# Attention units in a mixed attention and expert kernel: the product with V a pair later, three probability buffers, even units normalised by ScalarE and VectorE, and a shorter check of the low halves

## The reference, cut to what matters

```python
q, k, v = (layernorm(x) @ (codes * scales) + b)          # [16, 256, 16 heads, 128]
scores = einsum('bqhd,bkhd->bhqk', q, k) / sqrt(128)
attn = softmax(scores, axis=-1)
out = einsum('bhqk,bkhd->bqhd', attn, v) @ (wo_codes * wo_scales) + bo
x = x + layernorm(out)
logits = layernorm(x) @ gate.T                           # softmax, best 3 of 8 groups, best 6 experts
y = sum_k topk_w[k] * expert_k(layernorm(x)) + shared(layernorm(x))
x = x + layernorm(y)
```

## Time and profile before

| | value |
|---|---|
| three timed runs | 1329.47, 1331.55, 1333.42 us (median 1331.55) |
| profiled execution, span | 1341.9 us |
| PE busy | 1207.5 us (90%) |
| PE weight loads busy | 844.1 us (63%) |
| DVE busy | 860.6 us (64%) |
| ACT busy | 825.8 us (62%) |
| POOL busy | 931.0 us (69%) |

### The profile page before, as it was taken

How to read it: one execution, slowest core, us unless ns; L and a number is a source line. 1 busy time by engine, 2 the same in 40 slices (tenths; PEclk the granted TensorE clock), 3 DMA queues, 4 the chain that set the end, 5 groups by cost and what they waited for, 6 DMA issues and landing times.

```text
span 1341.9 us, 25318 instructions
## 1 busy us (share of the span) xinstructions
PE 1207.5 (90%) x7852; PEld 844.1 (63%) x7852; DVE 860.6 (64%) x2297; ACT 825.8 (62%) x2128; POOL 931.0 (69%) x1130
## 2 busy tenths in 40 slices
PE   4889999999999999989999999998958799989995
PEld 1556666666666666657666666665635378777973
DVE  5898567687678768767876876777676233222226
ACT  3666678768777776877777677777745133223413
POOL 4896456678878877986888798688764624444557
PEclk9899999999999999999999999999989899999998
DMA  7774987755555354354534545434445359898676
GB/s 257 173 191 94 228 211 150 163 102 120 122 99 118 73 116 94 73 108 82 93 68 98 97 69 94 79 70 81 81 100 165 112 166 259 226 234 213 131 211 227
DMA packets 364678, 182.68 MB, mean 136 GB/s; under 512 B 287440, under 2 KB 343222, under 8 KB 364544
## 3 DMA queue, kind: packets, MB, share of 16 engines
q1 hardware_dynamic: 344960, 166.18, 52.5%
q0 software_dynamic: 16416, 11.70, 4.9%
q10 hardware_dynamic: 3168, 3.15, 0.7%
HBM read 75.32 MB, written 64.69 MB: 104 GB/s over the span
## 4 chain that ended last, share of the span: by engine, by line
PE 39%; DVE 18%; DMA 14%; POOL 13%; issue 7%; ACT 5%; another core or an unknown queue 2%; SPq 1%; ACTq 0%; POOLq 0%; DVEq 0%
DMA PT<-PH 8%; PE bank L1066 7%; PE bank L1037 6%; PE bank L1081 6%; DMA Y<-W,wix 5%; POOL PH L972 4%; POOL P L967 4%; PE bank L1052 4%; PE bank L1098 3%; PE bank L1206 3%; DVE nm L1455 3%; PE bank L1219 2%; POOL BUF L716 2%; PE bank L1130 2%
## 5 line engine op out<-in xcount | busy, mean ns | idle before, releaser
L967 POOL TENSOR_SCALAR P<-P,rr 128x256 f32<-128x256 f32 x512 | 249.2, 498 | 141.2 <-DVE rr L1451 132.2
L1308 ACT ACTIVATE P<-bank,nm 128x256 f32<-128x256 f32 x512 | 237.2, 468 | 149.2 <-DVE nm L1455 140.9
L972 POOL TENSOR_TENSOR PH<-P,PH 128x512 f16<-128x512 f32 x256 | 296.2, 1171 | 20.1 <-ACT PH L1317 19.1
L1037 PE MATMUL bank<-RB,W 128*128 128x512 f16 x1076 | 257.9, 382 | 7.2 <-ACT Sx L645 4.2
L716 POOL DMA_INDIRECT BUF<-RT,ix x192 | 197.8, 1030 | 91.3 <-issue 42.2
L1066 PE MATMUL bank<-RB 128*128 128x256 f32 x1024 | 245.7, 383 | 2.7 <-issue 2.5
L1081 PE MATMUL bank<-PT,RB 128*128 128x256 f16 x1536 | 197.2, 273 | 36.1 <-DMA PT<-PH 32.1
L1455 DVE TENSOR_REDUCE nm<-bank 128x2 f32<-128x512 f32 x256 | 174.3, 682 | 51.1 <-PE bank L1066 50.5
L1081 PEld LDWEIGHTS bank<-PT,RB 128*128 128x128 f16 x1536 | 145.1, 98 | 95.9 <-DMA PT<-PH 50.5
L1066 PEld LDWEIGHTS bank<-RB 128*128 128x128 f32 x1024 | 185.7, 191 | 26.2 <-issue 3.8
L1317 ACT ACTIVATE PH<-P 128x512 f16<-128x512 f32 x256 | 161.4, 630 | 55.7 <-POOL P L967 38.9
(11 more groups left out here) (207 smaller groups left out, 1600.0 us busy)
## 6 DMA issues: line engine op xcount, KB each, us to landing
RB<-in_ewT SPq DMA_DIRECT2D x24, 352.0 KB
BUF<-zrow SPq DMA_DIRECT2D x4, 1926.0 KB, 8.4
W<-BUF SPq DMA_DIRECT2D x64, 120.4 KB
HT<-in_ewT SPq DMA_DIRECT2D x18, 352.0 KB
HT<-in_wc SPq DMA_DIRECT2D x24, 256.0 KB, 4.3
HT<-in_ws SPq DMA_DIRECT2D x24, 256.0 KB, 4.7
Y<-zrow SPq DMA_DIRECT2D x10, 512.0 KB, 3.5
RB<-in_ewd SPq DMA_DIRECT2D x24, 176.0 KB
```

Of the source, the lines that this page charges most:

```text
L967: r = eng.tensor_scalar(p, p, rr[:, w % 4, t:t + 1], SP_, ALU.mult, ALU.mult)
L972: eng.tensor_tensor(PH[:, w % 2, 1, :], P[:, w % 2, :], PH[:, w % 2, 0, :], ALU.subtract).then_inc(s["pl"], 1)
L1037: r = eng.matmul(bk_[:, :], W[:, m, a, c * 2048 + h * 128:c * 2048 + (h + 1) * 128], XT[:, bp % 2, b, c, :], start=(k == 0), stop=(k == n ...
L1308: r = eng.activation(P[:, u % 2, t * 256:(t + 1) * 256], bS[u % 2][:, t * 256:(t + 1) * 256], ACT.Exp, bias=nm0[:, u % 4, t:t + 1], accum_ ...
```

## The change

The order of TensorE has the product with V at lags 4 and 3 instead of 2 and 1, ahead of V's projection, and the output projection at lag 6, one unit in the even slot and one at the end of the odd slot. O high moves to lag 5 on ScalarE, O low to lag 6 on VectorE. PH and PT get a third buffer each, in the tile SSf, and all three are taken by the unit's number modulo three. The down weights of the shared expert, which had stood in SSf since slot 48, are loaded at slot 232 into XN.

Even units are no longer normalised in P. VectorE makes a scaled reciprocal `r64`; ScalarE rounds with it as a per-row scale (two instructions of 256 columns); VectorE makes the low half from P, `r64` and the high half (two instructions). Odd units go as before (GpSimd, ScalarE, GpSimd).

The check of the weights' low halves is a maximum per weight block (`tensor_reduce` to one column) instead of the bitwise and/or into a 256-word tile. All of ORDER, PLACE, W_AT, PE_AT, STORE_AT and KEEP_AT are written anew; END becomes 263.

```diff
-W_AT = (0, 0, 1, 2, 2, 3, 4, 5, 5, 6, 7, 7, 8, 9, 10, 10, 11, 12, 12, 13, 14, 15, 15, 16)
+W_AT = (0, 0, 1, 2, 2, 3, 5, 5, 6, 7, 8, 9, 9, 10, 11, 13, 13, 13, 13, 14, 16, 16, 16, 17)
-ORDER = {
-    "pe": ([("S", 0), ("S", -1), ("Q", -2), ("K", -2), ("WO", 4), ("WO", 3), ("V", -6), ("PV", 2), ("PV", 1),
-                ("bg", 0)],
-           [("bg", 0)]),
-    "act": ([("exp", 0), ("bg", 0), ("exp", -1)],
-           [("Q", -1), ("P", 1), ("V", -5), ("P", 0), ("O", 3), ("bg", 0)]),
-    "dve": ([("max", 0), ("O", 4), ("max", -1), ("bg", 0), ("recip", 0), ("bg", 0), ("bg", 0)],
-           [("bg", 0), ("recip", 0), ("K", -1), ("bg", 0), ("V", -5), ("bg", 0)]),
-    "pool": ([("bg", 0)],
-           [("norm", 1), ("norm", 0), ("P", 1), ("P", 0), ("bg", 0)]),
+NPT = 3
+ORDER = {'pe': ([('S', 0), ('S', -1), ('Q', -2), ('K', -2), ('PV', 4), ('PV', 3), ('V', -6), ('WO', 6), ('bg', 0)],
+        [('bg', 0), ('WO', 6)]),
+ 'act': ([('bg', 0), ('exp', 0), ('exp', -1), ('bg', 0), ('Q', -2)],
+         [('P', 1), ('V', -5), ('P', 0), ('bg', 0), ('O', 5), ('bg', 0)]),
+ 'dve': ([('max', 0), ('O', 6), ('max', -1), ('bg', 0), ('recip', 0), ('scale', 0), ('bg', 0)],
+         [('recip', 0), ('K', -1), ('bg', 0), ('P', 1), ('bg', 0), ('V', -5)]),
+ 'pool': ([('bg', 0)], [('norm', 0), ('bg', 0), ('lo', 0), ('bg', 0)]),
...
-PE_AT = (17, 19, 23, 31)
-STORE_AT = (18, 20)
+PE_AT = (19, 20, 25, 33)
+STORE_AT = (18, 18)
...
+        SSh = SSf[:, :].bitcast(F16)
+        PHB = [PH[:, 0, :, :], PH[:, 1, :, :], SSh[:, 0:1024].rearrange("p (l n) -> p l n", l=2)]
+        PTB = [PT[:, 0, :, :, :, :], PT[:, 1, :, :, :, :],
+               SSh[:, 1024:2048].rearrange("p (l t c q) -> p l t c q", l=2, t=2, c=2)]
...
-        sdf = SSf[:, 0:768].rearrange("p (j n) -> p j n", j=3)
+        sdf = XN[:, 0:3, :]
...
-                if n == 0:
-                    eng.tensor_scalar(lowbits, lo.bitcast(U32), NOSIGN, None, ALU.bitwise_and).then_inc(s["lf"], 1)
-                else:
-                    eng.wait_ge(s["lf"], n)
-                    eng.scalar_tensor_tensor(out=lowbits, in0=lo.bitcast(U32), scalar=NOSIGN, in1=lowbits,
-                                             op0=ALU.bitwise_and, op1=ALU.bitwise_or).then_inc(s["lf"], 1)
+                eng.tensor_reduce(lowmax[:, n:n + 1], lo.bitcast(U32), AX, ALU.max).then_inc(s["lf"], 1)
...
-                eng.wait_ge(s["pl"], w + 1)
-                if w >= 2:
-                    eng.wait_ge(s["pv"], w - 1)
+                eng.wait_ge(s["pld" if w % 2 == 0 else "plp"], w // 2 + 1)
+                if w >= NPT:
+                    eng.wait_ge(s["pv"], w - NPT + 1)
...
             def p_high(w):
-                eng.wait_ge(s["pn"], w + 1)
-                if w >= 2:
-                    eng.wait_ge(s_pt[w % 2], 16 * (w // 2))
-                eng.activation(PH[:, w % 2, 0, :], P[:, w % 2, :], ACT.Copy).then_inc(s["ph"], 1)
+                if w >= NPT:
+                    eng.wait_ge(s_pt[w % NPT], 16 * (w // NPT))
+                hi = PHB[w % NPT][:, 0, :]
+                if w % 2 == 0:
+                    eng.wait_ge(s["rs"], w // 2 + 1)
+                    for t in range(2):
+                        r = eng.activation(hi[:, t * 256:(t + 1) * 256], P[:, 0, t * 256:(t + 1) * 256],
+                                           ACT.Copy, scale=r64[:, w % 4, t:t + 1])
+                else:
+                    eng.wait_ge(s["pn"], w // 2 + 1)
+                    r = eng.activation(hi, P[:, 1, :], ACT.Copy)
+                r.then_inc(s["ph"], 1)
...
+            def scale(w):
+                eng.wait_ge(s["r"], w + 1)
+                eng.tensor_scalar(r64[:, w % 4, :], rr[:, w % 4, :], SP_, None, ALU.mult).then_inc(s["rs"], 1)
+
+            def p_low(w):
+                eng.wait_ge(s["rs"], w // 2 + 1)
+                eng.wait_ge(s["ph"], w + 1)
+                for t in range(2):
+                    n = slice(t * 256, (t + 1) * 256)
+                    r = eng.scalar_tensor_tensor(out=PHB[w % NPT][:, 1, n], in0=P[:, 0, n],
+                                                 scalar=r64[:, w % 4, t:t + 1], in1=PHB[w % NPT][:, 0, n],
+                                                 op0=ALU.mult, op1=ALU.subtract)
+                r.then_inc(s["pld"], 1)
```

More of the change, by code:

```diff
@@ L41 @@
 RSQRT_MAGIC = float(0x5F3759DF)
-NOSIGN = 0x7FFF7FFF
 FAR = 1.0e6
@@ L108 @@
 X_SHIFT = 12
-PE_AT = (17, 19, 23, 31)
-STORE_AT = (18, 20)
+PE_AT = (19, 20, 25, 33)
+STORE_AT = (18, 18)
 PROLOGUE = {"act": "wxwwxwxww", "dve": "xxxxxxxxxxxxxxxxxwxwxwwww"}
[L112 to L123, removed]
[6 rows of a table removed]
[L130 to L136, removed]
+KEEP_AT = (22, 34)
+PLACE = {'x': {'dve': ((1, 2), (1, 2), (2, 0), (2, 2), (2, 4), (2, 6), (3, 4), (4, 4), (4, 4), (4, 5), (4, 6), (7, 2),
+               (7, 4), (8, 3), (8, 6), (9, 2), (9, 4), (12, 0), (14, 0)),
+       'act': ((9, 5), (9, 5), (10, 0), (10, 3), (11, 3), (13, 2)),
+       'pool': ()},
[7 rows of a table added]
+       'act': ((11, 4), (11, 5), (11, 5), (12, 0), (17, 2), (17, 3), (17, 5), (18, 0), (19, 5), (21, 5),
+               (25, 5)),
+       'pool': ((12, 0), (12, 0), (12, 0), (13, 0), (36, 0), (38, 0), (39, 1), (39, 2), (42, 0), (43, 0),
+                (46, 0), (47, 0), (48, 0), (49, 1), (50, 0), (51, 3), (54, 0), (55, 0), (55, 2), (57, 0),
+                (57, 0), (57, 3), (58, 0), (58, 0), (59, 0), (59, 3), (60, 0), (62, 0))}}
 def places(chain, base):
@@ L252, in build @@
         rr = sb("rr", [128, 4, 2])
+        r64 = sb("r64", [128, 4, 2])
         st = sb("st", [128, 2, 4, 6])
@@ L284, in build @@
         Lt = C1
-        lowbits = C1[:, :, :].rearrange("p t e -> p (t e)").bitcast(U32)
+        lowmax = C1[:, 0, 0:32]
         low1, low2 = Ms[:, 32:33], Ms[0:1, 33:34]
@@ L345, in build @@
         lix = sb("lix", [64, 1], U32)
-        names = ("c0 cg cd gt S e r pn ph pl pv oh ol wo q ql k kl v vh vl xc po wm wh wl "
+        names = ("c0 cg cd gt S e r rs pn ph pld plp pv oh ol wo q ql k kl v vh vl xc po wm wh wl "
                  "lf lc xr fo hd bi yi dd lb sw swh swl sg ssl saf sah sal sdn sy et ebt eg esl eac eo eow wix wt wtc fa fp fd fs fn fb fx fy").split()
@@ L351, in build @@
         s_st = [sem(f"s_st{i}") for i in range(NST)]
-        s_pt = [sem(f"s_pt{i}") for i in range(2)]
+        s_pt = [sem(f"s_pt{i}") for i in range(NPT)]
         s_x1 = [sem(f"s_x1{i}") for i in range(2)]
@@ L558, in rows @@
                 eng.wait_ge(s["lf"], 32)
-                return eng.tensor_reduce(low1, lowbits, AX, ALU.max)
+                return eng.tensor_reduce(low1, lowmax, AX, ALU.max)
             LC.step("dve", FLAG_AT, rows)
@@ L849, in _ @@
                                       ).then_inc(s["sw"], 16)
+                if slot == 232:
+                    eng.wait_ge(s["xc"], XC.n)
                     eng.dma_start(sdf[:, 0:2, :], sdT[0:256, :].rearrange("(j p) n -> p j n", p=128)
@@ L884, in _ @@
             eng.wait_ge(s["swl"], 4)
-            eng.wait_ge(s["pl"], NU)
+            eng.wait_ge(s["pld"], NI)
+            eng.wait_ge(s["plp"], NI)
             eng.wait_ge(s["xc"], XC.n)
-            for k in range(2):
-                eng.wait_ge(s_pt[k], 16 * NI)
+            for k in range(NPT):
+                eng.wait_ge(s_pt[k], 16 * len(range(k, NU, NPT)))
             eng.wait_ge(s["pv"], NU)
@@ L968, in norm, with p_low_plain @@
                 r.then_inc(s["pn"], 1)
-            def p_low(w):
+            def p_low_plain(w):
                 eng.wait_ge(s["ph"], w + 1)
-                eng.tensor_tensor(PH[:, w % 2, 1, :], P[:, w % 2, :], PH[:, w % 2, 0, :], ALU.subtract
-                                  ).then_inc(s["pl"], 1)
+                eng.tensor_tensor(PHB[w % NPT][:, 1, :], P[:, w % 2, :], PHB[w % NPT][:, 0, :], ALU.subtract
+                                  ).then_inc(s["plp"], 1)
             for u in SLOTS:
-                slot_work("pool", u, {"norm": norm, "P": p_low, "bg": lambda *a: run_plan("pool", eng, *a),
+                slot_work("pool", u, {"norm": norm, "lo": p_low_plain, "bg": lambda *a: run_plan("pool", eng, *a),
                                       "at": at_place("pool", eng)})
@@ L1075, in pv @@
                     eng.wait_ge(s["vl"], 4 * (i // 4 + 1))
-                eng.wait_ge(s_pt[u % 2], 16 * (u // 2 + 1))
+                eng.wait_ge(s_pt[u % NPT], 16 * (u // NPT + 1))
                 eng.wait_ge(s["ol"], i)
@@ L1082, in pv @@
                                        V[:, i // 4 % 2, a, 2 * q + kc, h % 4 * 128:(h % 4 + 1) * 128],
-                                       PT[:, u % 2, b, :, kc, :], start=(k == 0), stop=(k == 5))
+                                       PTB[u % NPT][:, b, :, kc, :], start=(k == 0), stop=(k == 5))
                         k += 1
@@ L1305, in exp @@
                 if u >= 2:
-                    eng.wait_ge(s["pl"], u - 1)
+                    eng.wait_ge(s["pld" if u % 2 == 0 else "plp"], u // 2)
                 for t in range(2):
```

(2 more changed lines are left out.)

5 lines of the change are left out of this document (2 added, 3 removed), and 16 rows, old and new, of tables (ORDER, PLACE).

## The result

The changed kernel took 1461.97 us (median of 4 runs, 1460.12 to 1464.27) against 1330.51 us before: 1.098 times, 95% interval 1.0956 to 1.1005. It is slower by 131 us, where 33 us less were forecast, and far outside the stated range of 1268 to 1322 us. Its profiled execution spans 1460.9 us.

The account below looks back on a forecast made before the run. TensorE was taken as the bound, with 66 us of stalls in the middle. The terms -33 + 0 + 7 - 6 - 1 gave -33 us, from 1331.55 to 1298 us; range 1268 to 1322, the forecast's own 1283 to 1309.

Parts of the forecast that it names:

- part 4: Weight check and first batch pair: shorter check instructions and less GpSimd work, -6 us, bounds -10 and +5.
- Rival (d): The change doesn't do what it says: transfers blocked on SP's queue keep products late, 1330 us; chance 0.06.
- Part 1: Middle of attention: product with V a pair later removes TensorE's waits for transposed probabilities, -33 us, from -27 to -40.
- Part 2: TensorE's 12 us of stalls for O low stay, under another line; counted 0, from -12 to +12.
- Part 3: Even units: work leaves GpSimd; VectorE gets 0.87 us a pair more, less 0.35 of waiting for GpSimd, reaching 5.8.
- The 87% against 73% for VectorE: VectorE's busy share of a pair in the middle, forecast after the change against before.
- The +7 us for VectorE's lateness: Middle: busier VectorE stalls TensorE ten or so times more where steps pile up, +7 us, bounds -12 and +40.
- rival (a): Most stalls go, if VectorE's lateness was mostly GpSimd's doing: -65 us in all, 1267 us; chance 0.13.
- The half rate of a scalar_tensor_tensor: VectorE's new low halves: 0.5 us a pair more by the skill's page; L539's time showed no half rate.

Follow-up runs that it names:

- the masked kernel: The changed kernel with the old check of the weights' low halves, sign bits masked, put back: 1287.51 us, 0.967 of before.
- the later product alone: Kernel before, its own places, with only the product with V a pair later, three buffers, O and output projection moved along: 1319.22 us, 0.980.
- the new places without the split: Changed kernel with the old masked check, but GpSimd again normalises and takes the low half of all units: 1330.54 us, 0.988.
- the split on the old places: Kernel before with even units' normalising and low half moved from GpSimd to ScalarE and VectorE, down weights loaded late: 1348.64 us, 1.004.
- both parts on the old places: Kernel before, its places and weight slots kept, with product with V a pair later and even units taken partly off GpSimd: 1340.86 us, 0.996.

## Why the prediction was wrong

**The step that failed is part 4**, "31 L546 of 879 ns become reductions like L559, 407 ns". As a duration this was right: the new L537 took 420 ns. But the check's result decides which code TensorE runs from slot 24 on, and I took that result as unchanged. The diff shows that the sign mask goes; I read the edit as one of durations. At stake were 1.73 us of each pair, three times all stalls of the middle. Rival (d), the change that doesn't do what it says, was priced for SP's queue (+4) and never for the branch.

The other steps are judged by the masked kernel, which is the change as it was forecast except for the shorter check. Its stretches against those of the kernel before, in profiles:

| stretch | forecast | profiles |
|---|---|---|
| first twelve pairs | -6 | -4.0 |
| middle | -33 + 7 = -26 | -50.0 |
| last scores to last projection | -1 | +4.0 |
| what follows, the same work | 0 | -8.8, not due to the change |

- **The sum**: -33 us were forecast, 1298; measured -44, 1287.5 on a chip at 1331.4. Direction and range would have held, and the size was a quarter short. That it came so near is partly luck: the middle gave nearly twice what was forecast, and the end of attention lost where it was to gain.
- **Part 1** (-33 us, bound -27 to -40): all waits for the transposed tile went, in the masked kernel and in the later product alone. Alone, it gave 0.020 x 1331 = 26 us, just under the low end; 7.6 us more of waits stand at O low in that kernel.
- **Part 2** (O's 12 us stay): the wait for O low did move in front of the product with V. With the whole change it went from 9.6 to 7.1 us, near the 0 that was taken; with the move alone it grew to 17.2.
- **Part 3**: VectorE was to be at 5.8 us a pair and was at 657.95/115 = 5.72; GpSimd at 3.5, and was at 408.73/115 = 3.55; ScalarE at 5.84, and was at 5.57, with a high half of 513 ns instead of 588. That VectorE's figure came out is luck, since two errors cancel. The new instructions cost more: the low halves 94.2 us for some 103 pairs in 700 us (L1469, with those written to the third buffer), `scale` 18.6, together 1.09 us a pair instead of 0.87. And more of VectorE's waiting for GpSimd went: 5.30 + 1.09 - 5.72 = 0.67 us a pair instead of 0.35, of which 0.22 had gone with the later product and the new places, before the split (584.58/115 = 5.08). By line, the small step of rows 8 went from a mean of 326 ns to 172 with the split (339 without it on the same places). L680 went from 1394 to 425, and for that either is enough, the new places without the split (425) or the split on the old places (418). The 87% against 73% for VectorE also set a pair of 6.68 against one of 7.26; against 6.68 both times it is 87% and 79%.
- **The +7 us for VectorE's lateness** did not come. 66 us of stalls were there, about 16 are left, so 50 went instead of the 26 that -33 and +7 make for the middle. For the middle, rival (a), that most stalls go with GpSimd's hold (-33 - 12 - 10), was nearer than the forecast, though it too went by places: with both parts on the old places the lateness came in full (24.8 us of waits for O low, where 9.6 were).
- **The half rate of a scalar_tensor_tensor** with two SBUF sources that aren't bf16, the rule of the Trainium skill (Vector Engine (DVE) Microarchitecture Reference, Points that are easy to get wrong) weighed under part 3, does not show: 497 ns for 256 columns less 424 for a plain instruction leaves 73, not 250. With both parts on the old places the same instruction's mean is 625 ns; its median stays at 483 there, and its longest is 1466, as in the collision above.
- **Part 4**, its value (-6 for the first batch pair): with the mask, so without the shorter check, the first twelve pairs lost 4.0 us; with the raw maximum in the changed kernel 5.5. In the kernel before, the raw maximum alone left them at 111.45 us, against 111.67. So the check's 14.6 us of VectorE's time were worth next to nothing to TensorE.
- **Part 5** (-1, bounds -4 and +3): wrong in sign and outside its bounds, 20.6 us instead of 16.6. The deferred work did not fill gaps: in the masked kernel TensorE is busy 15.6 us of the 20.6, in the kernel before 13.5 of 16.6, and three waits for O low, 3.9 us, stand in it.

## What to carry to other kernels

When an edit touches the value that a branch, a loop bound or a table is chosen by, price both outcomes before its cost: here 15 us of VectorE's time (an estimate) stood against 199 us of TensorE's. A test for zero on raw words is not a test for zero; it needs the sign masked off, above all for differences of a value and its rounded self. An absolute value takes the sign off too, but then the way from the maximum to the flag must not lose fractions. A run that only shows the fast code doesn't test such a check: it needs data for which the slow code has to run. When profiles of two kernels are compared, compare a stretch with the same code as well: here it differed by more than 8 us, and hid that the end of attention had become 4 us longer. And parts of a tuned schedule do not add: the same split cost 1.6% on one set of places and gained 2.1% on another, so a part is judged only with the places that belong to it.

## What the runs showed of the hardware that I had not expected

- ScalarE's Copy with a scale turns -0 into +0 where VectorE's multiplication keeps it, as far as the code that ran tells: same data, three passes and 1462 us with the high half from ScalarE, two passes and 1312.6 us (on a slower chip) with it from VectorE.
- A reduction with one operand in SBUF did not wait for GpSimd. In the kernel before with the new check, 22 of its 32 reductions lie wholly inside a GpSimd instruction, and all take 419 to 421 ns. The masked step, with two operands there, took up to 1380:

```profile
L542 DVE TENSOR_REDUCE C<-W x32: 419/420/421, 11.9 to 118.4; 128x1 f32<-128x256 uint32 x32
```
```profile
L546 DVE SCALAR_TENSOR_TENSOR C<-W,C x31: 424/583/1380, 17.6 to 122.2; 128x256 uint32<-128x256 uint32 x31
```
